# The state's part of y computed earlier and accumulated in y's own bank, in a chunked selective-state block

## What is computed

```python
y_intra = einsum(sg, dg, xgc) + einsum(sb, dg, xbc)           # within a chunk of tokens
_, Sprev = jax.lax.scan(step, 0, (cdec, st))                   # state carried from chunk to chunk
y_inter = SCALE * einsum('bclgn,bclge,bcgenp->bclgep', Cc, dec_in, Sprev)
y = (y_intra + y_inter).reshape(B, T, D_INNER)
y = _rms(y * jax.nn.silu(z))
return y @ W_out
```

## Time and profile before

| | before |
|---|---|
| median of 3 runs | 256.66 us (256.44 to 256.72) |
| profiled execution, own time | 257.01 us |
| its span, first to last instruction | 255.2 us |
| PE busy | 223.2 us, 87% |
| DVE busy | 210.0 us, 82% |
| ACT busy | 188.1 us, 74% |
| POOL busy | 162.8 us, 64% |

### The profile page before, as it was taken

How to read it: one execution, slowest core, us unless ns; L and a number is a source line. 1 busy time by engine, 2 the same in 40 slices (tenths; PEclk the granted TensorE clock), 3 DMA queues, 4 the chain that set the end, 5 groups by cost and what they waited for, 6 DMA issues and landing times.

```text
span 255.2 us, 6621 instructions
## 1 busy us (share of the span) xinstructions
PE 223.2 (87%) x1962; PEld 174.8 (68%) x1962; DVE 210.0 (82%) x646; ACT 188.1 (74%) x724; POOL 162.8 (64%) x279
## 2 busy tenths in 40 slices
PE   0895899688999998999999999999999999997930
PEld 0893444467788777868878886887688868755930
DVE  1779999987688987975998999889899987975762
ACT  2356748769987789876887797799769976977742
POOL 7433125666789698685868686867586775567351
PEclk9999689999999999999999999999999999999995
DMA  5980000000000000000000001000100100011023
GB/s 121 222 267 0 3 0 0 1 0 4 3 3 3 0 3 1 3 0 5 4 0 3 0 5 41 3 0 11 35 4 0 45 0 3 0 42 37 8 57 77
DMA packets 10199, 6.45 MB, mean 25 GB/s; under 512 B 864, under 2 KB 9856, under 8 KB 10160
## 3 DMA queue, kind: packets, MB, share of 16 engines
q1 hardware_dynamic: 10016, 5.77, 9.5%
q0 software_dynamic: 144, 0.21, 0.4%
HBM read 3.88 MB, written 2.10 MB: 23 GB/s over the span
## 4 chain that ended last, share of the span: by engine, by line
PE 48%; ACT 18%; issue 12%; DVE 11%; POOL 7%; DMA 2%; ACTq 1%; DVEq 0%; POOLq 0%
PE bank L979 9%; PE bank L1060 5%; PE bank L973 5%; PE pair L967 5%; PE bank L881 5%; ACT dt_all L747 4%; ACT bt L686 3%; PE bank L848 3%; PE bank L1120 2%; PE bank L1119 2%; ACT bank L675 2%; ACT junk L664 2%; PE bank L1096 2%; PE bank L1099 2%; DMA w_sb<-w_in 2%
## 5 line engine op out<-in xcount | busy, mean ns | idle before, releaser
L675 ACT ACTIVATE bank<-bank,rsn 128x512 f32<-128x512 f32 x32 | 21.1, 661 | 20.9 <-PE bank L881 20.8
L1377 DVE TENSOR_TENSOR x<-bank,wx 128x512 f32<-128x512 f32 x32 | 21.9, 684 | 16.6 <-ACT bank L675 13.6
L979 PE MATMUL bank<-x,sg 64*64 64x256 f32 x256 | 34.6, 385 | 0.0
L979 PE MATMUL bank<-xg,sg 64*64 64x256 f32 x256 | 33.8, 376 | 0.0
L967 PE MATMUL pair<-x,turned_bc 64*64 64x256 f32 x224 | 29.6, 376 | 0.0
L547 POOL TENSOR_TENSOR y<-ysum,zs 128x256 f32<-128x256 f32 x32 | 23.5, 734 | 6.3 <-DVE ysum L1400 6.2
L973 PE MATMUL bank<-st,bt 64*64 64x256 f32 x128 | 20.8, 395 | 5.9 <-ACT bt L686 5.0
L455 POOL TENSOR_TENSOR rb<-mse,halfn 128x2 f32<-128x2 f32 x32 | 23.5, 735 | 2.5
L452 POOL TENSOR_TENSOR mse<-msb,eps_all 128x2 f32<-128x2 f32 x32 | 8.0, 250 | 26.1 <-ACT junk L666 26.0
L979 PEld LDWEIGHTS bank<-xg,sg 64*64 64x64 f32 x256 | 21.4, 133 | 4.8
L427 POOL TENSOR_TENSOR x_lo<-xnT_all,x_hi 128x128 fp32r<-128x128 f32 x32 | 14.7, 460 | 14.8 <-ACT x_hi L590 14.8
(11 more groups left out here) (195 smaller groups left out, 763.4 us busy)
## 6 DMA issues: line engine op xcount, KB each, us to landing
x_all<-x SPq DMA_DIRECT2D x16, 128.0 KB, 4.3
out<-o_all SPq DMA_DIRECT2D x14, 128.0 KB, 2.5
cm<-consts SPq DMA_DIRECT2D x1, 640.0 KB, 5.4
w_sb<-w_in SPq DMA_DIRECT2D x1, 480.0 KB, 4.4
out<-o_all SPq DMA_DIRECT2D x4, 64.0 KB, 2.2
cm<-consts POOLq DMA_DIRECT2D x1, 128.0 KB, 4.2
wo_sb<-w_out SPq DMA_DIRECT2D x1, 128.0 KB, 4.8
bcb_sb<-bc_bias SPq DMA_DIRECT2D x1, 96.0 KB, 3.8
```

Of the source, the lines that this page charges most:

```text
L675: nc.scalar.activation(x_ps[:], x_ps[:], ACT.Silu, scale=rsn[:, par:par + 1]).then_inc(S["x_silu"], 1)
L979: mm = nc.tensor.matmul(y_ps[half(h)], sg[half(h), a, r], rx(x, r)[half(h)], start=start, stop=stop)
L1377: vec.tensor_tensor((x1, xg)[a][:, par].rearrange("p (a e) -> p a e", e=P), x_ps[:].rearrange("p (a e) -> p a e", e=P), wx[:, par, a].unsq ...
```

## The change

`from_state` writes into `y_ps`, the bank of y, and opens the accumulation there; all products of `within_chunk` add to it. It moves in PE's step from the head of `mix`, behind `project_bc` and `y_turn`, to a place of its own ahead of `project_bc`, behind `turn`. It waits there for the gated y of the tile before (`y_ready`), since that frees the bank. `inter_ps`, `zt`, `ysum`, ACT's copy, DVE's sum and POOL's product go; DVE multiplies `y_ps` by the gate and writes y.

```diff
-            def gated(n, q, par):
-                pool.wait_ge(S["ysum_ready"], n + 1)
...
-                nc.gpsimd.tensor_tensor(y[:, par], ysum[:, par], zs[:, q], ALU.mult).then_inc(S["y_ready"], 1)
...
-            def state_part(n, par):
-                act.wait_ge(S["inter_ps"], n + 1)
...
-                nc.scalar.activation(zt[:, par], inter_ps, ACT.Copy).then_inc(S["zt_sb"], 1)
...
             def turn(n, q):
                 pe.wait_ge(S["bc_turned"], n + 1)
                 pe.wait_ge(S["t_sb"], n)
-                pe.wait_ge(S["zt_sb"], max(n - 1, 0))
...
-            def from_state(to, par, state):
+            def from_state(par, state, stop):
                 for h in range(2):
-                    mm = nc.tensor.matmul(to[half(h)], bt[half(1 - h), par, h, half(h)], state[half(1 - h)], start=True,
-                                          stop=True)
+                    mm = nc.tensor.matmul(y_ps[half(h)], bt[half(1 - h), par, h, half(h)], state[half(1 - h)], start=True,
+                                          stop=stop)
...
-            def mix(n, q, par):
+            def state_part(n, q, par):
 
                 if n >= NQ:
                     pe.wait_ge(S["st_ready"], n - NQ + 1)
                 else:
                     pe.wait_ge(S["st_zero"], 2)
+                pe.wait_ge(S["t_sb"], n + 1)
+                pe.wait_ge(S["y_ready"], n)
+                from_state(par, st[:, q], False).then_inc(S["inter_ps"], 1)
+
+            def mix(n, q, par):
+
+                if n < NQ:
                     pe.wait_ge(t_turn[1], 3)
-                pe.wait_ge(S["t_sb"], min(n + 2, NT))
-                from_state(inter_ps, par, st[:, q]).then_inc(S["inter_ps"], 1)
+                pe.wait_ge(S["inter_ps"], n + 1)
                 pe.wait_ge(S["x1_ready"], n + 1)
-                pe.wait_ge(S["ysum_ready"], n)
...
-                    within_chunk(0, r, x1[:, par], start=(r == 0), stop=False)
+                    within_chunk(0, r, x1[:, par], start=False, stop=False)
...
                 if n + 1 < NT:
                     turn(n + 1, (n + 1) % NQ)
+                if within(n) and not general:
+                    state_part(n, q, par)
                 if n + 2 < NT:
                     project_bc(n + 2, par)
...
-            def summed_y(n, par, general):
+            def gated_y(n, q, par, general):
                 dve.wait_ge(S["y_ps"], n + 1)
-                if not general:
-                    dve.wait_ge(S["zt_sb"], n + 1)
+                dve.wait_ge(S["zec_ready"], n + 1)
                 if not isinstance(n, int) or n >= 2:
-                    dve.wait_ge(S["y_ready"], n - 1)
-                vec.tensor_tensor(ysum[:, par], y_ps, yk[:] if general else zt[:, par],
-                                  ALU.add).then_inc(S["ysum_ready"], 1)
+                    dve.wait_ge(S["yt_ps"], n - 1)
+                    dve.wait_ge(S["ysq_done"], n - 1)
...
+                vec.tensor_tensor(y[:, par], yk[:] if general else y_ps, zs[:, q], ALU.mult).then_inc(S["y_ready"], 1)
```

More of the change, by code:

```diff
@@ L160, in build @@
         zbc_ps, x_ps = bank[0], bank[1]
-        t_ps, inter_ps = bank[2][:, 0:DI], bank[2][:, DI:]
+        t_ps = bank[2][:, 0:DI]
         yt_ps, o_ps, fk_ps = bank[3][:, 0:DI], bank[3][:, DI:DI + D], bank[3][:, DI + D:DI + D + H]
@@ L250, in build @@
         junk_o = sb("junk_o", 128, D)
-        zt = sb("zt", 128, 2, DI)
-        ysum = sb("ysum", 128, 2, DI)
         msb = sb("msb", 128, 2, R)
@@ L272, in build @@
         names = ("x_hi x_lo zbc_ps x_ps bc_ready rotated bc_turned rs_now x_silu z_silu sq_done mse_ready rb_ready w_ready "
-                 "zec_ready x1_ready xg_ready t_ps t_sb sg_ps sg_ready p_ps p_added st_ready inter_ps zt_sb y_ps ysum_ready y_ready ysq_done "
+                 "zec_ready x1_ready xg_ready t_ps t_sb sg_ps sg_ready p_ps p_added st_ready inter_ps y_ps y_ready ysq_done "
                  "yt_ps yt_sb o_ps o_sb st_zero weights").split()
@@ L528, in last_ffn @@
                 carry(6)
-                gated(NT - 1, NQ - 1, 1)
                 factors(7)
@@ L540, in last_ffn @@
                     rstd(k)
-            def gated(n, q, par):
-                pool.wait_ge(S["ysum_ready"], n + 1)
-                if not isinstance(n, int) or n >= 2:
-                    pool.wait_ge(S["yt_ps"], n - 1)
-                    pool.wait_ge(S["ysq_done"], n - 1)
-                nc.gpsimd.tensor_tensor(y[:, par], ysum[:, par], zs[:, q], ALU.mult).then_inc(S["y_ready"], 1)
             def step(n, q, general):
@@ L554, in step @@
                     early(n + 2, q % 2)
-                if within(n):
-                    gated(n, q, q % 2)
                 if within(n + 2):
@@ L704, in late_o @@
                                      accum_out=at(osq_all, i)).then_inc(S["o_sb"], 1)
-            def state_part(n, par):
-                act.wait_ge(S["inter_ps"], n + 1)
-                if not isinstance(n, int) or n >= 2:
-                    act.wait_ge(S["ysum_ready"], n - 1)
-                nc.scalar.activation(zt[:, par], inter_ps, ACT.Copy).then_inc(S["zt_sb"], 1)
             def empty_ffn_bank(n):
@@ L732, in step @@
                     late_yt(n - 1)
-                if within(n):
-                    state_part(n, q % 2)
                 if within(n + 2):
@@ L1022, in token @@
                     gate()
-                    from_state(y_ps, par, sk[:]).then_inc(G["y_ps"], 1)
+                    from_state(par, sk[:], True).then_inc(G["y_ps"], 1)
                     pe.wait_ge(G["x1k"], n + 1)
@@ L1033, in mix_general @@
                 pe.wait_ge(S["xg_ready"], i + 1)
-                pe.wait_ge(S["ysum_ready"], i)
-                pe.wait_ge(S["t_sb"], min(i + 2, NT))
+                pe.wait_ge(S["y_ready"], i)
                 wait_past(pe, G["st"], i * L)
@@ L1087, in project_k @@
                     pe.wait_ge(S["t_sb"], NT)
-                    pe.wait_ge(S["zt_sb"], NT)
                 elif u == 7:
@@ L1113, in project_r @@
                 elif u == 7:
-                    pe.wait_ge(S["ysum_ready"], NT)
+                    pe.wait_ge(S["y_ready"], NT)
                 else:
@@ L1392, in state @@
                 vec.tensor_tensor(sp[:], p_ps, st[:, q], ALU.add).then_inc(S["p_added"], 1)
-            def summed_y(n, par, general):
+            def gated_y(n, q, par, general):
                 dve.wait_ge(S["y_ps"], n + 1)
-                if not general:
-                    dve.wait_ge(S["zt_sb"], n + 1)
+                dve.wait_ge(S["zec_ready"], n + 1)
                 if not isinstance(n, int) or n >= 2:
-                    dve.wait_ge(S["y_ready"], n - 1)
-                vec.tensor_tensor(ysum[:, par], y_ps, yk[:] if general else zt[:, par],
-                                  ALU.add).then_inc(S["ysum_ready"], 1)
+                    dve.wait_ge(S["yt_ps"], n - 1)
+                    dve.wait_ge(S["ysq_done"], n - 1)
+                if general:
+                    vec.tensor_tensor(yk[:], y_ps, yk[:], ALU.add).then_inc(G["own"], 1)
+                    dve.wait_ge(G["own"], n + 1)
+                vec.tensor_tensor(y[:, par], yk[:] if general else y_ps, zs[:, q], ALU.mult).then_inc(S["y_ready"], 1)
             def tokens_general(i, q, par):
-                dve.wait_ge(S["ysum_ready"], i)
+                dve.wait_ge(S["y_ready"], i)
                 dve.wait_ge(S["x1_ready"], i + 1)
@@ L1522, in last_ffn @@
                     tokens_general(NT - 1, NQ - 1, 1)
-                summed_y(NT - 1, 1, general)
+                gated_y(NT - 1, NQ - 1, 1, general)
                 norm_biases(6)
@@ L1559, in step @@
                         tokens_general(n - 1, (q - 1) % NQ, (q + 1) % 2)
-                    summed_y(n - 1, (q + 1) % 2, general)
+                    gated_y(n - 1, (q - 1) % NQ, (q + 1) % 2, general)
                     if not general and carries(n - 1):
```

## The result

| | before | changed |
|---|---|---|
| median | 256.69 us (4 runs, 256.44 to 257.24) | 263.44 us (4 runs, 263.22 to 264.77) |
| span of the profiled execution | 255.2 us | 261.6 us |
| PE, DVE, ACT, POOL busy | 223.2, 210.0, 188.1, 162.8 us | 235.1, 208.2, 181.8, 142.6 us |

The account below looks back on a forecast made before the run. PE's list of work and its own waits were taken as the bound. +0.76 - 0.45 = +0.31 us over 27 tiles gave 8.4, less 0.74 for tiles 2 and 10: +7.6, so 264.3 us, range 258.0 to 267.5.

Parts of the forecast that it names:

- (a): PE's wait for ACT's `bt` ahead of the state's and the chunk's products goes: -0.45 us a tile.
- (b): The state's product moves between full-array matmuls, so `project_bc`'s weights load later, with two tiling-mode switches: +0.76 us a tile.
- (c): PE's new wait for `y_ready` ahead of the state's product: 0 in the steady stages, bounds 0 to 0.24 us.
- I count tile 1 as any other: In tile 1 the wait for y moves ahead of `project_bc` and both switches; its cost was taken as a usual tile's.
- 27 tiles at +0.31: The net loss of a usual tile, +0.76 - 0.45 us, taken over 27 tiles: 8.4 us.
- (d): ACT's copy and POOL's product go, DVE's sum becomes a product; all lie beside PE's work: 0.
- Hidden switches: Rival: `project_bc`'s weights load while the state's product runs: 255.0 us, 259 if half hidden; chance 0.17 for both.
- The new wait as the bound: Rival: ahead of `project_bc` PE waits for DVE's gated y: 270.8 us, 266 if one step of four; chance 0.08.
- the early tiles gain more: Rival: up to tile 10, POOL's relief brings x sooner and 2 us come back: 262 us; no separate chance given.

Follow-up runs that it names:

- two pairs: The changed kernel with the state's product made twice a tile: 278.00 us with both at its place, 285.49 us with the second behind `project_bc`.
- bank 5: The kernel before, with the state's product kept in its place but written into an idle part of bank 5, without PE's wait for `bt`: 248.57 us.
- the load put back: The changed kernel with idle work in the old places, a copy on ACT and a product on POOL that nobody reads: 264.35 us beside 264.48.
- the pairs apart: The changed kernel with the state's product made at its place and once more between `project_bc` and the transposes of y: 285.49 us, ratio 1.1162.
- in a row: The changed kernel with the state's product made twice at its place, one directly after the other: 278.00 us, ratio 1.0868.
- the product at the head of `mix`: The changed kernel with the state's product moved back behind the transposes of y, still opening y's bank: 261.41 us, ratio 1.0215.

## Why the prediction was right or wrong

**The size.** The forecast had the change at +7.6 us; between the medians it is 263.44 - 256.69 = 6.75, between the spans 6.4, and in the changed kernel's second set of runs, between medians, 264.48 - 255.96 = 8.5. The period of four tiles was forecast at 25.4 and is 25.43. From `project_x` to the first product of the chunk 2.70 was forecast and 2.69 measured: +0.30 for a tile against +0.31.

**(a), -0.45: the size was right, the reason only in part.** The first product of the chunk starts 0.31 us behind the first transpose of y, 0.47 sooner than before. But (a) and (b) were added as if each were there without the other. Putting the wait back costs nothing (264.10 beside 264.48), so in this order the move alone hides it. By itself, with another bank, removing the wait brought 7.4 us; the price of 0.45 came back, or most of it, in three tiles of four.

**(b), +0.76: right.** The weights of `project_bc` load 202.23 - 201.34 = 0.89 us behind the first transpose of `turn`, where it was 196.00 - 195.90 = 0.10: +0.79. The runs with two pairs divide such a price: 0.43 for the passes, 0.29 for the way in and out. The rule of the Trainium skill (TensorEngine Tiling (Array Packing), Key Properties), that changing the tiling mode drains TensorE, agrees. Between those two runs nothing differs but the place of the second pair, and the 0.29 us come with the two more changes of tile size.

**(c), 0 in the steady stages: right; "I count tile 1 as any other": the step that failed.** The first tiles by the distance of the starts of `project_x`: tile 1 took 5.65 us before and takes 6.57, +0.92 instead of +0.31, since DVE gates y only at 53.47 and `project_bc` and a switch stand behind it. Tiles 2 and 10 came out as forecast: 5.51 to 5.15 (-0.36, forecast -0.35) and 5.98 to 5.58 (-0.40, forecast -0.39).

**"27 tiles at +0.31": right for most of them.** From tile 11 to 29 every one lost 0.29 to 0.32. Tiles 6 to 9 were slower than their neighbours before (4.99, 4.98, 5.12 and 4.91 us, tile 5 4.83) and all take 5.14 or 5.15 now, so they lost 0.16, 0.16, 0.03 and 0.24: 4 x 0.31 - 0.59 = 0.65 less than the sum had, against 0.61 more in tile 1. That these two errors cancel is luck. Tile 0, counted at 0, is 0.23 shorter. From the `project_x` of step 0 to that of step 30 the time grew from 219.31 - 47.18 = 172.13 to 225.99 - 46.60 = 179.39 us, +7.26 against 7.6. The steps ahead are 47.18 - 46.60 = 0.58 us shorter, and what follows 35.89 - 35.61 = 0.28, both of which the forecast had at 0: together +6.4. These two, outside the steps that were reckoned, are most of its error against the spans. The first is scatter and not the change. All of it lies ahead of the program's first `project_x` (first row: before, second row: changed),

```profile
25.73 0.47 PE L881 MATMUL bank<-w_hi,x_hi 128*128 128x512 f32 x1 [2.75 <-DVE w_lo L1261]
...
25.15 0.76 PE L861 MATMUL bank<-w_hi,x_hi 128*128 128x512 f32 x1 [2.75 <-DVE w_lo L1244]
```

and from there to the `project_x` of step 0 all ten traces have 21.4 to 21.5 us. The start of that row lies between 24.38 and 25.15 in the nine others, those in bank 5 with the order of the kernel before among them (24.95 and 24.38): the trace of the kernel before came late to that row. Over the steps alone the change cost 7.26 us, and 179.87 - 172.13 = 7.74 by the changed kernel's second trace, on both sides of the 7.6 forecast.

**(d), 0: right**, shown by the load put back.

**The rivals.** Hidden switches fell: the pairs apart cost 7.5 us more than in a row. The new wait as the bound fell too: DVE's y holds PE up once. That the early tiles gain more is seen in tiles 2 and 10 alone, at the size that was forecast. Tile 30, counted at 0 for having no `project_bc`, did have a wait for `bt`: from `project_x` to the chunk's first product it takes 2.04 us where it took 2.38, and tile 31 then pays for the product's new place.

## What to carry to other kernels

A product on a part of the array is nearly free among its kind (it starts 0.01 to 0.02 us beside the others) and cost 0.72 to 0.76 us alone, between full-array work or ahead of products that the kernel makes wait for its end: count passes, switches and what has to start behind, not rows. When an engine bounds the kernel, work taken from the others is worth nothing (32 us of it, put back, changed nothing), while a wait of the bounding engine can be worth more than it looks in the list of waits: 5.0 us listed, 7.4 gained by another bank for one small result, 9.5 with two copies of ACT in another order. The starts had it at 0.45 a tile, some 13 us in 29 tiles as an estimate; part of the difference went into waits that came to light behind it. Find what the bounding engine waits for, and move the data (a bank) before the order; time of that engine spent on hiding its own wait is a loss when it is the longer of the two.

## What was not expected of the hardware

- In y's bank, ahead of the chunk's products, a product of the same tile size cost 0.72 us from its start to the first product behind it, about as much as between full-array matmuls (0.76), though no switch was added: the products behind it wait for its signal. PEld was idle for 0.52 us there, in the timeline of the kernel with the product at the head of `mix`:

```profile
201.09 0.14 PEld L958 LDWEIGHTS bank<-x,sg 64*64 64x64 f32 x2 [0.52 <-PE bank L952]
```

- At a change of tile size the idle time of PEld differs with what ran ahead. Ahead of 64x64 weights it is 0.17 us behind the transposes of 128 columns, and 0.30 behind `project_bc`'s 448 (pairs apart, first row). Ahead of full-array weights it is 0.39 behind the state's 256 columns, but only 205.24 - 205.17 = 0.07 behind `score`'s 64 (changed kernel, the rows after):

```profile
220.54 0.20 PEld L952 LDWEIGHTS bank<-st,bt 64*64 64x64 f32 x4 [0.30 <-issue]
...
204.61 0.56 PEld L937 LDWEIGHTS pair<-bt 64*64 64x64 f32 x7
205.24 0.52 PEld L1042 LDWEIGHTS bank<-wo_sb,yt 128*128 128x128 f32 x4
```

  So the 0.29 us of the way in and out belong to this product at these places; behind `score` the way out is shorter.
- Taking POOL's 23.5 us of products away lowered its busy time by only 20.2. Its power operation (`rb<-mse,halfn`, same size) went from 735 to 796 ns on average, 2.0 us in all. With the idle product put back behind it it took 733 again, but with bank 5, where the old product still stands behind it, 769; what sets it stays open.
